# Where the expert stage turns its rows: TensorE blocks through PSUM, or VectorE blocks of 32 by 32 in SBUF

## The chip, the core and the metric

One core of one Trainium2 chip runs the whole kernel as one program. TensorE (PE in the profile; its weight loads are PEld) multiplies, VectorE (DVE) and ScalarE (ACT) work on elements, GpSimd (POOL) issues the indexed transfers and SyncE (SP) the plain ones. The metric is the device time of one execution in microseconds (us), lower is better; the figure for a kernel is the median over runs.

## What is computed

A graph layer, a linear-attention mixer and then a mixture of experts over 1250 rows of 768 float32 numbers. Only the last matters here:

```python
probs = jax.nn.softmax(x @ router_w, axis=-1)
gates, idx = jax.lax.top_k(probs, TOPK_ROUTED)      # 8 experts, 2 for each row
gates = gates / jnp.sum(gates, axis=-1, keepdims=True)
g = jax.nn.silu(jnp.einsum('bsd,edh->bseh', x, w_gate))
u = jnp.einsum('bsd,edh->bseh', x, w_up)
expert_out = jnp.einsum('bseh,ehd->bsed', g * u, w_down)
routed = jnp.einsum('bse,bsed->bsd', dense_g, expert_out)
return alpha * shared + (1.0 - alpha) * routed
```

## The kernel before

The expert stage is the last third of the kernel, from about 1028 us of the span on. The rows picked for the experts have been written to DRAM in order of expert (`expert_in`), in 23 tiles (NTM) of 128 slots; the two halves of a tile (HP = 64 slots) may belong to two experts, whose weights lie in two sets of SBUF buffers.

What TensorE does with tile j (`tile` in `ffn_pe`): the gate product into banks 0 and 1, the up product into banks 2 and 3, then the down product into banks 4 and 5. Each product has two column blocks of 384 and six row blocks of 128 (KD = 6), and each of these is a pair of matmuls, one for each half of the slots (`product`). In gate and up the column block is the outer loop, in down the row block is. So a tile has 36 pairs, six times six: two sixths for gate (blocks 0 and 1), two for up, and two for down (rows 0 to 2, then 3 to 5). Down needs the gated rows as columns and gate needs the fetched rows as columns, and TensorE makes both by transposes: `h_transposes(j, 0)` turns the first half of the gated rows `hh` into bank 0, `x_transposes(j + 1)` the next tile's fetched rows `xgb` into banks 6 and 7, `h_transposes(j, 1)` the second half into bank 1. They stand between up and down, twelve of 128 by 128 in all. Three sorts of copies take them to SBUF: L885 (ScalarE, two for each tile, to `xgT`), L896 (ScalarE, to the first half of `hT`) and L1165 (VectorE, to the second half).

ScalarE further fetches the rows of tile j + 2 (`load_x`, L880) and applies Silu to the gate blocks (L894). VectorE multiplies the two up blocks by that (`take_h`, L1160) and adds the down result into rows of the output that GpSimd fetches (`add_rows`, L1173, two instructions for each half h). On GpSimd the two halves of a tile go strictly one after the other, since both may name the same output row: gather half 0 (L698), wait for the addition, scatter (L702), and only when that has landed gather half 1, wait for its addition, scatter. An addition waits for its gather, and half 0 also for the down product.

All engines run in order. VectorE's program is written out tile by tile: two `take_h`, the copy L1165, `add_rows(j, 0)`, `add_rows(j, 1)`. Weights of another expert are fetched by SyncE (L661) as soon as the last tile that uses the old ones is through gate, up or down. The names of semaphores that show below: `h_ready` (multiplication done), `hT_psum`, `hT_copied_act`, `hT_copied_dve` (turned and copied), `slot_xT_sb` (turned rows of a tile in SBUF), `out_rows_in` (gather landed), `y_psum` (down done), `y_added` (additions done).

Of the kernel before, what the change touches and what calls it, by code (L numbers as in the profile page):

```python
# [31 lines left out]
P = 128  # L32
# [24 lines left out]
def gps_layer(nc, x, src, dst, norm_g, norm_b, W1, a_src1, a_dst1, b1, W2, a_src2, a_dst2, b2, Wu, bu,  # L57
# [25 lines left out]
    with ExitStack() as ctx:  # L83
        def sem(name):
            return ctx.enter_context(nc.semaphore(name))
# [472 lines left out]
        s_g = sem("gate_psum")  # L558
        s_up = sem("up_psum")
        s_slot_xT = sem("slot_xT_psum")  # L560
        s_ht = sem("hT_psum")
        s_y = sem("y_psum")
        s_silu = sem("silu_ready")
        s_xTs = sem("slot_xT_sb")
        s_h = sem("h_ready")
        s_hTa = sem("hT_copied_act")
        s_hTs = sem("hT_copied_dve")
        s_yd = sem("y_added")
        s_last = sem("last_step")
        s_fout = sem("out_rows_written")  # L570
# [141 lines left out]
        def ffn_pe(pe, xf_turn):  # L712
# [85 lines left out]
                            ins.then_inc((s_g, s_up, s_y)[2 * i + k], 1)  # L798
                    ins.then_inc(s_slot_xT, 1)

            def h_transposes(j, b, i):

                pe.wait_ge(s_h, 2 * j + 1 + i)
                for k in range(3):
                    ins = tp.transpose(ps[i][:, k * P:(k + 1) * P], hh[:, b, (3 * i + k) * P:(3 * i + k + 1) * P], ident)
                ins.then_inc(s_ht, 1)

            def product(bank, frm, b, k, i, n):

                for h in range(2):  # L810
# [4 lines left out]
            def tile(j, b):  # L815

                loads = pe.value_load(loads_i[0:1, bass.ds(j, 1)], min_val=32, max_val=16 * (NB1 + 2))
                pe.wait_ge(s_xTs, 2 * j + 2)
                for m in range(2):
                    pe.wait_ge(s_ew[m], loads)  # L820
                    for i in range(2):
                        for k in range(KD):
                            ins = product(2 * m + i, xgT, b, k, m, i)
                        ins.then_inc((s_g, s_up)[m], 1)
                h_transposes(j, b, 0)
                if not (isinstance(j, int) and j == NTM - 1):
                    x_transposes(j + 1, 1 - b)
                else:
                    pe.wait_ge(s_last, 1)
                    tp.transpose(ps[6][:, 0:P], rows_f.to_broadcast([P, P]), ident).then_inc(s_slot_xT, 1)  # L830
                h_transposes(j, b, 1)
                pe.wait_ge(s_ew[2], loads)
                if not (isinstance(j, int) and j == 0):
                    pe.wait_ge(s_yd, 4 * j)
                for k in range(KD):
                    if k == 0:
                        pe.wait_ge(s_hTa, j + 1)
                    if k == 3:
                        pe.wait_ge(s_hTs, j + 1)
                    for o in range(2):  # L840
                        ins = product(4 + o, hT, b, k, 2, o)
                ins.then_inc(s_y, 1)
# [8 lines left out]
        def ffn_act(act):  # L851
            def take_xf(t):
                act.wait_ge(s_xt, 2 * (NT + t) + 1)
                sc.activation(xfT[:, 0:3, t * T:(t + 1) * T], ps[4][:, 0:3 * T].rearrange("p (k n) -> p k n", k=3),
                              ACT.Copy).then_inc(s_xta, 1)

            act.wait_ge(s_stats, 5)
            sc.activation(std[0:T, 0:5], mv[0:T, 0:5, 1], ACT.Sqrt, bias=epst[0:T]).then_inc(s_std, 1)
            for t in range(3):
                take_xf(t)  # L860
            act.wait_ge(s_stats, 6)
            sc.activation(std[0:T, 5:NT], mv[0:T, 5:NT, 1], ACT.Sqrt, bias=epst[0:T]).then_inc(s_std, 1)
            for t in range(NT):
                if t + 3 < NT:
                    take_xf(t + 3)
                act.wait_ge(s_sgp, t + 1)
                sc.activation(sg_s[0:T, t], ps[t % 2][0:T, 0:HS], ACT.Silu).then_inc(s_ssil, 1)
            act.wait_ge(s_exin, 1)
            sc.activation(ex[0:T], ex[0:T], ACT.Exp)
            sc.activation(ex2[0:T], ex2[0:T], ACT.Exp).then_inc(s_exout, 1)  # L870
            act.wait_ge(s_sgb, 16)
            sc.activation(alpha[0:T], lg[0:T, :, NE], ACT.Sigmoid, bias=sgb[0:T]).then_inc(s_exout, 1)
            for t in range(NT):
                act.wait_ge(s_shT, t + 1)
# [12 lines left out]

            def tile(j, b):
                last = isinstance(j, int) and j == NTM - 1
                if not (isinstance(j, int) and j + 2 >= NTM):  # L890
                    load_x(j + 2, b)
                for i in range(2):
                    act.wait_ge(s_g, 2 * j + 2 + i)
                    sc.activation(gs[:, b, i * 384:(i + 1) * 384], ps[i][:, 0:384], ACT.Silu).then_inc(s_silu, 1)  # L894
                act.wait_ge(s_ht, 2 * j + 1)
                sc.activation(hT[:, b, 0:3].rearrange("p k n -> p (k n)"), ps[0][:, 0:384], ACT.Copy).then_inc(s_hTa, 1)  # L896
                if not last:
                    take_x(j + 1, 1 - b)
                else:
                    act.wait_ge(s_h, 2 * j)  # L900
                    act.wait_ge(s_y, j + 2)
                    sc.activation(gs[:, 1, 0:384], ps[4][:, 0:384], ACT.Copy).then_inc(s_last, 1)

            act.wait_ge(s_rows, 16 * 2 * NT)
            load_x(0, 0)
            load_x(1, 1)
            take_x(0, 0)
            over_tiles(act, tile)

        def ffn_dve(dve, step, add_out, mean_var):  # L910
# [241 lines left out]
            for t in range(NT - 3, NT):  # L1152
                shared_out(t)

            def take_h(j):
                b = j % 2
                for i in range(2):
                    dve.wait_ge(s_silu, 2 * j + 1 + i)
                    dve.wait_ge(s_up, 2 * j + 2 + i)
                    dv.tensor_tensor(hh[:, b, i * 384:(i + 1) * 384], ps[2 + i][:, 0:384], gs[:, b, i * 384:(i + 1) * 384],  # L1160
                                     ALU.mult).then_inc(s_h, 1)

            def take_hT(j):
                dve.wait_ge(s_ht, 2 * j + 2)
                dv.tensor_copy(hT[:, j % 2, 3:6].rearrange("p k n -> p (k n)"), ps[1][:, 0:384]).then_inc(s_hTs, 1)  # L1165

            def add_rows(j, h):
                if h == 0:
                    dve.wait_ge(s_y, j + 2)
                dve.wait_ge(s_accin, 16 * (2 * j + h + 1))  # L1170
                for o in range(2):
                    cols = accb[0:HP, h, o * 384:(o + 1) * 384]
                    stt(out=cols, in0=ps[4 + o][HP * h:HP * h + HP, 0:384], scalar=slot_info[0:HP, j, h, 0:1], in1=cols,  # L1173
                        op0=ALU.mult, op1=ALU.add).then_inc(s_yd, 1)

            def last_rows():

                dve.wait_ge(s_slot_xT, 2 * NTM + 1)
                dv.tensor_scalar(same, ps[6][:, 0:P], rows_f[:, 0:1], info_last[:, 0:1], ALU.is_equal, ALU.mult).then_inc(s_last, 1)
                dve.wait_ge(s_h, 2 * NTM - 2)  # L1180
                dve.wait_ge(s_y, NTM + 1)
                dv.tensor_copy(gs[:, 1, 384:768], ps[5][:, 0:384]).then_inc(s_last, 1)
                dve.wait_ge(s_accin, 16 * (2 * NTM - 1))
                for o in range(2):
                    dve.wait_ge(s_last, 5 + o)
                    cols = accb[:, 0, o * 384:(o + 1) * 384]
                    dv.tensor_tensor(cols, cols, ps[7 - o][:, 0:384], ALU.add).then_inc(s_yd, 1)

            for j in range(NTM - 1):
                take_h(j)  # L1190
                take_hT(j)
                if j == 0:
                    dve.wait_ge(s_infoin, 32)
                    dv.tensor_copy(rows_f, info_last[:, 1:2].bitcast(I32)).then_inc(s_last, 1)
                    dve.wait_ge(s_last, 1)
                add_rows(j, 0)
                add_rows(j, 1)
            take_h(NTM - 1)
            take_hT(NTM - 1)
            last_rows()  # L1200


# [1301 lines left out]
```

## Time and profile before

| | us |
|---|---|
| median of 3 runs | 1628.32 |
| lowest, highest | 1626.89, 1630.79 |
| span of the profiled execution, first to last instruction | 1625.5 |

The span is 2.8 us below the median; what a sum makes of the span is added to the median. In the profile a line of a timeline gives the start and the duration of merged instructions of one line of code, and in brackets how long the engine had been idle and what ended that. TensorE's durations overlap each other, since matmuls are pipelined: the distance between starts is what counts there.

### The profile page before, as it was taken

What the parts mean: (1) busy time and instruction counts of PE and PEld (TensorE: products, weight loads), DVE (VectorE), ACT (ScalarE), POOL (GpSimd) and SP (SyncE); (2) the same over time, 40 slices, a digit from 0 to 9 for tenths busy, and PEclk for the clock granted to TensorE, in tenths of its full rate; (3) what the DMA queues carried; (4) which work ended last, traced back from release to release, by engine and by line L of the source; (5) the groups of instructions that cost most, each with busy time, mean ns of one, the idle gap of its engine ahead of it and who ended that gap; (6) DMA issues with size and microseconds to landing.
All of it is one profiled execution on the core that took longest, in us unless ns stands there. A gap on an engine that the chain in (4) does not pass through costs nothing.

```text
span 1625.5 us, 21891 instructions
## 1 busy us (share of the span) xinstructions
PE 1541.0 (95%) x8438; PEld 1021.0 (63%) x8439; DVE 820.7 (50%) x1552; ACT 335.3 (21%) x493; POOL 252.9 (16%) x236
## 2 busy tenths in 40 slices
PE   5999999999989999999879999899999999999996
PEld 3566666557779999999876555444444444444442
DVE  8655457988867889984997243111111111111111
ACT  3321111002222345560481210100000000001000
POOL 1187810000000000000000037011111111111111
PEclk9999999999999999999999999999999999999998
DMA  9900010000004536213111337925629211613450
GB/s 269 344 2 2 2 62 1 1 1 2 1 19 121 140 80 190 59 24 85 46 33 59 146 69 161 328 66 188 222 55 320 92 48 53 213 40 112 153 203 21
DMA packets 85339, 163.81 MB, mean 101 GB/s; under 512 B 18874, under 2 KB 48816, under 8 KB 85001
## 3 DMA queue, kind: packets, MB, share of 16 engines
q1 hardware_dynamic: 66903, 119.07, 22.6%
q0 software_dynamic: 12096, 23.27, 6.3%
q10 hardware_dynamic: 6258, 20.40, 4.5%
q8 instruction: 48, 0.79, 0.2%
q14 instruction: 34, 0.28, 0.1%
HBM read 127.75 MB, written 37.56 MB: 102 GB/s over the span
## 4 chain that ended last, share of the span: by engine, by line
PE 66%; DVE 12%; POOL 8%; issue 6%; DMA 5%; SPq 1%; DVEq 1%; ACT 1%; POOLq 0%
PE bank L811 31%; PE bank L1636 7%; POOL slot_table L1332 7%; PE bank L1674 6%; PE bank L1538 5%; PE bank L1595 3%; PE bank L721 2%; DVE arena L2396 2%; PE bank L1474 2%; DVE arena L2365 2%; PE bank L1722 1%; DMA arena<-in_L_ffn_w_down_dram 1%; DMA expert_in<-arena 1%; POOL expert_in L679 1%; DVE arena L2341 1%
## 5 line engine op out<-in xcount | busy, mean ns | idle before, releaser
L811 PE MATMUL bank<-arena 128*64 128x384 f32 x3312 | 541.1, 488 | 3.7 <-DMA arena<-in_L_ffn_w_down_dram 3.1
L811 PEld LDWEIGHTS bank<-arena 128*64 128x64 f32 x3312 | 237.1, 137 | 296.0 <-issue 291.8
L1173 DVE SCALAR_TENSOR_TENSOR arena<-bank,arena 64x384 f32<-64x384 f32 x88 | 50.3, 610 | 355.2 <-DMA arena<-out_dram,arena 200.7
L1674 PE MATMUL bank<-arena 125*125 125x198 f32 (+1 forms) x1200 | 188.9, 317 | 13.5 <-DVE arena L2365 13.3
L1674 PEld LDWEIGHTS bank<-arena 125*125 125x125 f32 x1200 | 182.1, 191 | 18.2 <-DVE arena L2365 17.9
L1636 PE MATMUL bank<-arena 128*125 128x192 f32 x960 | 161.9, 326 | 0.0
L1636 PEld LDWEIGHTS bank<-arena 128*125 128x125 f32 x960 | 156.1, 188 | 0.2
L1332 POOL DMA_INDIRECT slot_table<-arena x80 | 110.7, 1384 | 93.8 <-issue 93.8
L2202 DVE TENSOR_TENSOR arena<-arena,bank 125x417 f32 x186 | 109.4, 588 | 27.1 <-PE bank L1474 18.9
L672 POOL MEMSET arena<- 1x2500 f32 x1 | 2.2, 2179 | 597.0 <-DVE arena L2348 597.0
L2396 DVE SCALAR_TENSOR_TENSOR arena<-arena 125x1250 f32<-125x1250 f32 x60 | 90.8, 1514 | 4.2 <-ACT arena L1911 4.2
L1538 PE MATMUL bank<-arena 128*125 128x396 f32 x240 | 92.9, 496 | 0.0
L894 ACT ACTIVATE arena<-bank 128x384 f32<-128x384 f32 x46 | 22.6, 492 | 338.8 <-PE bank L811 338.8
L1924 ACT ACTIVATE arena<-arena 125x1250 f32<-125x1250 f32 x60 | 74.7, 1245 | 83.0 <-DVE arena L2396 81.5
L1595 PE MATMUL bank<-arena 128*128 128x250 f32 x360 | 89.7, 374 | 1.7 <-DVE arena L2255 1.7
L2365 DVE SCALAR_TENSOR_TENSOR arena<-arena 125x1250 f32<-125x1250 f32 x60 | 87.1, 1453 | 0.9 <-PE bank L1674 0.9
L2341 DVE CUSTOM_DVE_ANT_0 arena<-arena 125x1250 bf16<-125x1250 bf16 x60 | 86.6, 1454 | 0.0
L702 POOL DMA_INDIRECT out_dram<-arena x44 | 40.4, 918 | 295.9 <-DVE arena L1173 283.1
L1911 ACT ACTIVATE arena<-arena 125x1250 f32<-125x1250 f32 x60 | 79.5, 1335 | 27.0 <-DMA arena<-score_rows 19.4
L1422 PE MATMUL bank<-arena 128*125 128x384 f32 x240 | 82.5, 497 | 0.0
L1450 PE MATMUL bank<-arena 128*125 128x384 f32 x240 | 80.4, 487 | 0.0
L1160 DVE TENSOR_TENSOR arena<-bank,arena 128x384 f32<-128x384 f32 x46 | 25.6, 558 | 99.2 <-PE bank L811 98.9
(302 smaller groups left out, 1564.6 us busy)
## 6 DMA issues: line engine op xcount, KB each, us to landing
arena<-in_L_ffn_w_gate_dram SPq DMA_DIRECT2D x9, 2304.0 KB, 8.9
arena<-in_L_ffn_w_up_dram SPq DMA_DIRECT2D x9, 2304.0 KB, 10.3
arena<-in_L_ffn_w_down_dram SPq DMA_DIRECT2D x9, 2304.0 KB, 8.8
arena<-score_rows ACTq DMA_DIRECT2D x18, 585.9 KB
expert_in<-arena SPq DMA_DIRECT2D x23, 384.0 KB, 10.2
arena<-expert_in ACTq DMA_DIRECT2D x23, 384.0 KB, 3.7
arena<-in_L_mix_w_qkv_dram SPq DMA_DIRECT2D x2, 2304.0 KB, 17.2
xn_columns<-arena SPq DMA_DIRECT2D x1, 3750.0 KB, 15.6
```

Source lines behind the costliest of these rows:

```text
L811: ins = tp.matmul(ps[bank][HP * h:HP * h + HP, 0:384], frm[:, b, k, HP * h:HP * h + HP], ew[h][i][:, k, n * 384:(n + 1) * 384], start=(k = ...
L1332: pl.indirect_dma_start(table_dram[:, :], bass.IndirectOffsetOnAxis(ap=slot_i[0:T, c:c + 1], axis=0), vhw[0:T, NTB * TC + c:NTB * TC + c + ...
L1422: ins = tp.matmul(ps[i % 2][0:T, 0:384], xnT[:, k, t * T:(t + 1) * T], wkv[:, 0, k, hf * 384:(hf + 1) * 384], start=(k == 0), stop=(k == K ...
L1450: ins = tp.matmul(ps[2 + hf][0:T, 0:384], xnT[:, k, t * T:(t + 1) * T], wkv[:, 1, k, hf * 384:(hf + 1) * 384], start=(k == 0), stop=(k == ...
L1538: ins = tp.matmul(ps[q % 4][0:T, 0:2 * VW], xnT[:, k, t * T:(t + 1) * T], w12x[:, k, 2 * hf:2 * hf + 2, :], start=(k == 0), stop=(k == KD ...
L1595: ins = tp.matmul(ps[q % 2][:, 0:QN], wq[:, k, mb * P:(mb + 1) * P], xnT[:, k, g * QN:(g + 1) * QN], start=(k == 0), stop=(k == KD - 1))
L1636: ins = tp.matmul(ps[side_bank(u)][0:T, 0:FW], frm[:, k, t * T:(t + 1) * T], wchunk[:, c % 2, k, :], start=(k == 0), stop=(k == KD - 1))
L1674: ins = tp.matmul(ps[bank][0:T, c * width:(c + 1) * width], ptile[0:T, j % NPT, dt * T:(dt + 1) * T], values(n - first, st), start=(st == ...
L2202: dv.tensor_tensor(o, o, ps[6 + j % 2][0:T, 0:G], ALU.add).then_inc(s_acc, 1)
L2341: step(dv.tensor_tensor_reduce(junk[0:T, dt % 2], mask[0:T, dt], srowb[0:T, n % 2], 1.0, -3.0e38, ALU.add, ALU.max, smax[0:T, dt:dt + 1]))
L2365: stt(out=ptile[0:T, j % NPT], in0=tbuf[0:T, j % NTB3], scalar=1.0, in1=counts[0:T, st, 0:N], op0=ALU.min, op1=ALU.mult).then_inc(s_pt, 1)
L2396: stt(out=tbuf[0:T, j % NTB3], in0=abbuf[0:T, n % 2, 1], scalar=ssrc[:, st:st + 1], in1=tbuf[0:T, j % NTB3], op0=ALU.add, op1=ALU.max).the ...
```

## The change

Of tile 0 the fetched rows are still turned by TensorE and copied by ScalarE. All others, and all gated rows, are turned by VectorE, 32 by 32 blocks at a time, from SBUF to SBUF: an instruction takes one strip of 32 partitions (rows r*32 on) and, of each 128 columns, the block number f, and writes to partitions f*32 on. For a strip there are four such instructions, for 128 rows sixteen: 32x96 elements each for half of the gated rows (3 blocks), 32x192 for the fetched rows (6 blocks). TensorE's transposes and the copies L885 (but for tile 0), L896 and L1165 are gone.

VectorE's tile j now is: multiply, 16 turns, multiply, 16 turns, the 16 turns of the fetched rows of tile j + 2 (`turn_x`), `add_rows(j, 0)`, `add_rows(j, 1)`. The down product's first half waits for `hT_sb` at the first 16 turns, its second half at the second 16.

```diff
             def tile(j, b):
...
-                h_transposes(j, b, 0)
-                if not (isinstance(j, int) and j == NTM - 1):
-                    x_transposes(j + 1, 1 - b)
...
-                h_transposes(j, b, 1)
                 pe.wait_ge(s_ew[2], loads)
...
                 for k in range(KD):
-                    if k == 0:
-                        pe.wait_ge(s_hTa, j + 1)
-                    if k == 3:
-                        pe.wait_ge(s_hTs, j + 1)
+                    if k % 3 == 0:
+                        pe.wait_ge(s_hTs, 2 * j + 1 + k // 3)
...
+            Q = 32
+
+            def turn_blocks(to, rows, r):
+
+                for f in range(P // Q):
+                    frm = rows[r * Q:(r + 1) * Q].rearrange("p (k f c) -> p f k c", f=P // Q, c=Q)[:, f]
+                    ins = dv.transpose(to[f * Q:(f + 1) * Q, :, r * Q:(r + 1) * Q], frm)
+                return ins
...
                     dv.tensor_tensor(hh[:, b, i * 384:(i + 1) * 384], ps[2 + i][:, 0:384], gs[:, b, i * 384:(i + 1) * 384],
                                      ALU.mult).then_inc(s_h, 1)
...
+                    dve.wait_ge(s_h, 2 * j + 1 + i)
+                    for r in range(P // Q):
+                        ins = turn_blocks(hT[:, b, 3 * i:3 * i + 3], hh[:, b, i * 384:(i + 1) * 384], r)
+                    ins.then_inc(s_hTs, 1)
+
+            def turn_x(j):
+                b = j % 2
+                dve.wait_ge(s_xg[b], 16 * (j // 2 + 1))
+                for r in range(P // Q):
+                    ins = turn_blocks(xgT[:, b], xgb[:, b], r)
+                ins.then_inc(s_xTd, 1)
...
+            turn_x(1)
             for j in range(NTM - 1):
                 take_h(j)
-                take_hT(j)
                 if j == 0:
...
+                if j + 2 < NTM:
+                    turn_x(j + 2)
                 add_rows(j, 0)
                 add_rows(j, 1)
```

VectorE, one tile of the middle of the stage (here L1160 multiplies, L1165 copies the turned half, L1173 adds; x2 is two instructions in a row). Before:

```order
L1160 TENSOR_TENSOR arena<-bank,arena 128x384 [waits up_psum,silu_ready] x2
L1165 COPY arena<-bank 128x384 [waits hT_psum]
L1173 SCALAR_TENSOR_TENSOR arena<-bank,arena 64x384 [waits out_rows_in,y_psum]
L1173 SCALAR_TENSOR_TENSOR arena<-bank,arena 64x384
L1173 SCALAR_TENSOR_TENSOR arena<-bank,arena 64x384 [waits out_rows_in]
L1173 SCALAR_TENSOR_TENSOR arena<-bank,arena 64x384
```

In the changed kernel (L1158 multiplies, L1150 turns, L1178 adds):

```order
L1158 TENSOR_TENSOR arena<-bank,arena 128x384 [waits up_psum,silu_ready]
L1150 STREAM_TRANSPOSE arena<-arena 32x3x32 [waits h_ready]
L1150 STREAM_TRANSPOSE arena<-arena 32x3x32 x15
L1158 TENSOR_TENSOR arena<-bank,arena 128x384 [waits up_psum,silu_ready]
L1150 STREAM_TRANSPOSE arena<-arena 32x3x32 [waits h_ready]
L1150 STREAM_TRANSPOSE arena<-arena 32x3x32 x15
L1150 STREAM_TRANSPOSE arena<-arena 32x6x32 [waits slot_rows_in0]
L1150 STREAM_TRANSPOSE arena<-arena 32x6x32 x15
L1178 SCALAR_TENSOR_TENSOR arena<-bank,arena 64x384 [waits out_rows_in,y_psum]
L1178 SCALAR_TENSOR_TENSOR arena<-bank,arena 64x384
L1178 SCALAR_TENSOR_TENSOR arena<-bank,arena 64x384 [waits out_rows_in]
L1178 SCALAR_TENSOR_TENSOR arena<-bank,arena 64x384
```

One copy has gone, and 48 turns have come in, 16 of them between the two multiplications and 32 between the second one and the additions.

TensorE from the up product on to the next gate product, at the same place. Before:

```order
L811 MATMUL bank<-arena 64x384 [waits expert_w1_in]
L811 MATMUL bank<-arena 64x384 x23
L805 MATMUL bank<-arena 128x128 [waits h_ready]
L805 MATMUL bank<-arena 128x128 x2
L796 MATMUL bank<-arena 128x128 [waits slot_rows_in0]
L796 MATMUL bank<-arena 128x128 x5
L805 MATMUL bank<-arena 128x128 [waits h_ready]
L805 MATMUL bank<-arena 128x128 x2
L811 MATMUL bank<-arena 64x384 [waits hT_copied_act,y_added,expert_w2_in]
L811 MATMUL bank<-arena 64x384 x11
L811 MATMUL bank<-arena 64x384 [waits hT_copied_dve]
L811 MATMUL bank<-arena 64x384 x11
```

In the changed kernel (`product` is L803):

```order
L803 MATMUL bank<-arena 64x384 [waits expert_w1_in]
L803 MATMUL bank<-arena 64x384 x23
L803 MATMUL bank<-arena 64x384 [waits hT_sb,y_added,expert_w2_in]
L803 MATMUL bank<-arena 64x384 x11
L803 MATMUL bank<-arena 64x384 [waits hT_sb]
L803 MATMUL bank<-arena 64x384 x11
```

Down now stands right behind up, and each of its halves waits for VectorE.

## Rows read from the trace of the kernel before

**Rows 1.** The page, part 1: busy time, share of the span, instructions.
```profile
PE 1541.0 (95%) x8438; PEld 1021.0 (63%) x8439; DVE 820.7 (50%) x1552; ACT 335.3 (21%) x493; POOL 252.9 (16%) x236
```

**Rows 2.** Timeline of PE: start, us, engine, line, tiles, count, [idle before]; one tile.
```profile
1150.41 23.44 PE L811 MATMUL bank<-arena 128*64 128x384 f32 x144
1173.78 0.55 PE L805 MATMUL bank<-arena 128*128 128x128 f32 x3
1174.16 0.82 PE L796 MATMUL bank<-arena 128*128 128x128 f32 x6
1174.82 0.49 PE L805 MATMUL bank<-arena 128*128 128x128 f32 x3
1175.24 23.44 PE L811 MATMUL bank<-arena 128*64 128x384 f32 x144
```

**Rows 3.** Timeline of DVE, one tile: additions of both halves, then the two multiplications.
```profile
1183.25 1.14 DVE L1173 SCALAR_TENSOR_TENSOR arena<-bank,arena 64x384 f32<-64x384 f32 x2 [7.34 <-PE bank L811]
1192.50 1.15 DVE L1173 SCALAR_TENSOR_TENSOR arena<-bank,arena 64x384 f32<-64x384 f32 x2 [8.12 <-DMA arena<-out_dram,arena]
1194.93 0.56 DVE L1160 TENSOR_TENSOR arena<-bank,arena 128x384 f32<-128x384 f32 x1 [1.27 <-PE bank L811]
1198.80 0.56 DVE L1160 TENSOR_TENSOR arena<-bank,arena 128x384 f32<-128x384 f32 x1 [3.31 <-PE bank L811]
```

**Rows 4.** Timeline of DVE, instructions queued with no wait between them: earlier stages.
```profile
223.53 0.35 DVE L2227 COPY arena<-bank 64x192 f32<-64x192 f32 x1
223.80 0.14 DVE L2228 COPY arena<-bank 64x3 f32<-64x3 f32 x1
223.96 0.36 DVE L2227 COPY arena<-bank 64x192 f32<-64x192 f32 x1
224.24 0.16 DVE L2228 COPY arena<-bank 64x3 f32<-64x3 f32 x1
...
951.12 0.15 DVE L1023 TENSOR_SCALAR arena<-arena 125x7 f32<-125x7 f32 x1
951.19 0.15 DVE L1024 TENSOR_SCALAR arena<-arena 125x7 f32<-125x7 f32 x1
```

**Rows 5.** Groups by line and shape: DVE from SBUF to SBUF; busy us, mean ns.
```profile
L2259 DVE COPY arena<-arena 125x80 f32<-125x80 f32 x1 | 0.2, 241 | 0.0
L1034 DVE TENSOR_TENSOR arena<-arena 125x196 f32<-125x196 f32 x1 | 0.4, 362 | 0.0
```

**Rows 6.** Timeline of DVE: the seven additions of half 1 that waited longest.
```profile
1121.29 1.15 DVE L1173 SCALAR_TENSOR_TENSOR arena<-bank,arena 64x384 f32<-64x384 f32 x2 [11.40 <-DMA arena<-out_dram,arena]
...
1170.28 1.15 DVE L1173 SCALAR_TENSOR_TENSOR arena<-bank,arena 64x384 f32<-64x384 f32 x2 [10.73 <-DMA arena<-out_dram,arena]
...
1248.88 1.15 DVE L1173 SCALAR_TENSOR_TENSOR arena<-bank,arena 64x384 f32<-64x384 f32 x2 [14.84 <-DMA arena<-out_dram,arena]
...
1272.56 1.15 DVE L1173 SCALAR_TENSOR_TENSOR arena<-bank,arena 64x384 f32<-64x384 f32 x2 [9.74 <-DMA arena<-out_dram,arena]
...
1422.56 1.16 DVE L1173 SCALAR_TENSOR_TENSOR arena<-bank,arena 64x384 f32<-64x384 f32 x2 [10.74 <-DMA arena<-out_dram,arena]
...
1521.41 1.15 DVE L1173 SCALAR_TENSOR_TENSOR arena<-bank,arena 64x384 f32<-64x384 f32 x2 [10.26 <-DMA arena<-out_dram,arena]
...
1571.43 1.15 DVE L1173 SCALAR_TENSOR_TENSOR arena<-bank,arena 64x384 f32<-64x384 f32 x2 [10.62 <-DMA arena<-out_dram,arena]
```

**Rows 7.** Timeline of PE around the longest of these waits.
```profile
1224.91 23.44 PE L811 MATMUL bank<-arena 128*64 128x384 f32 x144
1250.68 0.90 PE L805 MATMUL bank<-arena 128*128 128x128 f32 x3 [2.33 <-DVE arena L1160]
...
1253.43 23.68 PE L811 MATMUL bank<-arena 128*64 128x384 f32 x144
```

**Rows 8.** Stretches: us, busy PE, PEld, DVE, ACT, POOL, then PEclk, DMA share, GB/s.
```profile
1248.00:1250.60 2.60, 0.35 (x4) 0.00 (x0) 1.68 (x4) 0.00 (x0) 0.00 (x0) 0.99 0.92 238
1250.60:1253.40 2.80, 2.72 (x12) 2.42 (x12) 0.49 (x2) 1.48 (x3) 0.92 (x1) 0.50 1.02 410
1253.40:1256.50 3.10, 3.10 (x19) 1.42 (x20) 0.56 (x1) 0.00 (x0) 0.00 (x0) 0.91 1.04 408
```

More of the change, by code:

```diff
@@ L560, in gps_layer @@
         s_slot_xT = sem("slot_xT_psum")
-        s_ht = sem("hT_psum")
         s_y = sem("y_psum")
@@ L565, in gps_layer @@
         s_h = sem("h_ready")
-        s_hTa = sem("hT_copied_act")
-        s_hTs = sem("hT_copied_dve")
+        s_hTs = sem("hT_sb")
+        s_xTd = sem("slot_xT_turned")
         s_yd = sem("y_added")
@@ L799, in x_transposes @@
                     ins.then_inc(s_slot_xT, 1)
[L801 to L806, printed above, removed]
             def product(bank, frm, b, k, i, n):
@@ L817, in tile @@
                 loads = pe.value_load(loads_i[0:1, bass.ds(j, 1)], min_val=32, max_val=16 * (NB1 + 2))
-                pe.wait_ge(s_xTs, 2 * j + 2)
+                if isinstance(j, int) and j == 0:
+                    pe.wait_ge(s_xTs, 2)
+                else:
+                    pe.wait_ge(s_xTd, j)
                 for m in range(2):
@@ L824, in tile @@
                         ins.then_inc((s_g, s_up)[m], 1)
-                h_transposes(j, b, 0)
-                if not (isinstance(j, int) and j == NTM - 1):
-                    x_transposes(j + 1, 1 - b)
-                else:
+                if isinstance(j, int) and j == NTM - 1:
                     pe.wait_ge(s_last, 1)
                     tp.transpose(ps[6][:, 0:P], rows_f.to_broadcast([P, P]), ident).then_inc(s_slot_xT, 1)
-                h_transposes(j, b, 1)
                 pe.wait_ge(s_ew[2], loads)
@@ L890, in tile @@
                 if not (isinstance(j, int) and j + 2 >= NTM):
+                    if not (isinstance(j, int) and j == 0):
+                        act.wait_ge(s_xTd, j)
                     load_x(j + 2, b)
@@ L893, in tile @@
                     act.wait_ge(s_g, 2 * j + 2 + i)
+                    if i == 0 and not (isinstance(j, int) and j < 2):
+                        act.wait_ge(s_h, 2 * j - 2)
                     sc.activation(gs[:, b, i * 384:(i + 1) * 384], ps[i][:, 0:384], ACT.Silu).then_inc(s_silu, 1)
[L895 to L899, printed above, removed]
+                if last:
                     act.wait_ge(s_h, 2 * j)
@@ L1161, in take_h @@
                                      ALU.mult).then_inc(s_h, 1)
-            def take_hT(j):
-                dve.wait_ge(s_ht, 2 * j + 2)
-                dv.tensor_copy(hT[:, j % 2, 3:6].rearrange("p k n -> p (k n)"), ps[1][:, 0:384]).then_inc(s_hTs, 1)
+                    dve.wait_ge(s_h, 2 * j + 1 + i)
[8 more added lines that the diff above has]
+                ins.then_inc(s_xTd, 1)
             def add_rows(j, h):
@@ L1176, in last_rows @@
             def last_rows():
-                dve.wait_ge(s_slot_xT, 2 * NTM + 1)
+                dve.wait_ge(s_slot_xT, 3)
                 dv.tensor_scalar(same, ps[6][:, 0:P], rows_f[:, 0:1], info_last[:, 0:1], ALU.is_equal, ALU.mult).then_inc(s_last, 1)
@@ L1198, in ffn_dve @@
             take_h(NTM - 1)
-            take_hT(NTM - 1)
             last_rows()
```

## The prediction

> **What bounds the kernel now.** I read the page first: TensorE is busy 95% of the span, VectorE 50% [rows 1]. The share says only that TensorE is the one to relieve; what relief is worth is read in the stage itself. There the timeline of TensorE is regular: a stretch of products starts at 1150.41 and the next at 1175.24, so a tile takes 24.83 us, with the twelve transposes in the 1.46 us between 1173.78 and 1175.24 [rows 2]. TensorE never idles in such a tile. The timeline of VectorE gives the products' pace: the two multiplications start 3.87 us apart, which is one sixth of a tile's products [rows 3], so the products take 6 x 3.87 = 23.2 us and the transposes, with what they keep the queue from doing, 24.83 - 23.2 = 1.6 us. That is all that the change can take from TensorE.
>
> VectorE's own timeline is the one to study, since it gets the work. Its additions of half 0 start when down ends (1183.25), those of half 1 9.25 us later (1.13 of work and 8.12 of waiting for the scatter and the next gather), and end at 1193.65; the first multiplication starts at 1194.93, 11.68 after the down product's end, because up's first block is ready then [rows 3]. So VectorE has only 1.3 us of air between the last addition and the first multiplication, and in 7 of 22 tiles none: there the wait of half 1 is 9.74 to 14.84 us [rows 6].
>
> **What is removed.** 23 tiles' transposes on TensorE, all but the fetched rows of tile 0; taken alone 1.6 x 22 = 35 us. The copies on ScalarE are hidden now and give nothing; the 0.56 us copy on VectorE went to nobody's wait but the down product's second half.
>
> **What is added: the price of a turn.** 32 instructions of 32x96 and 16 of 32x192 for each tile, in the second half of a chain that TensorE waits for. The trace has no turn; the bounds come from the nearest rows.
> Duration: SBUF to SBUF, 125x80 took 241 ns and 125x196 took 362 ns [rows 5], that is 1.04 ns for each further column and 158 ns fixed; 96 columns are 258 ns, 192 are 358 ns.
> Distance between starts: that depends on what VectorE may overlap. Two instructions of 7 columns on the same partitions start 0.07 us apart although each lasts 0.15, and a 192-column copy lets the next one start after 0.27 of its 0.35 us. But where the copies go over from partitions 0 to 63 to partitions 64 to 127, the next one starts only when the last has ended: 223.80 + 0.14, next at 223.96 [rows 4]. So overlapped a turn costs 0.27 - (192 - 96) x 0.00104 = 0.17 us for 96 columns and 0.27 for 192; not overlapped 0.258 + 0.02 = 0.28 and 0.38. In `turn_blocks` f is the inner loop, so every instruction writes to another strip of 32 partitions than the one before it. I take the row with the change of partitions, since it is the nearer one. On top of that a block can hardly leave before its last of 32 columns has come in, 32 x 1.04 = 33 ns more, in full or not at all; I take a third of that: **0.29 us for 96 columns, 0.39 for 192**, and keep 0.28 and 0.31 for the range.
>
> The Trainium skill says the same of the overlap, and it speaks against this change: in "VectorE: DVE Perf Modes", section "Two Vector instructions with no wait between them", an instruction whose output starts in another quadrant (32 partitions) than the last output into that memory is held until all earlier ones are finished. Its section "The three transpose paths" gives 311 ns for 128x128 bf16 on VectorE. An estimate from that figure would be 311 less 32 x 1.04 = 278 ns, with the gap 0.30 us for 96 columns, and the sum below would be 10 us higher.
>
> **A tile of the changed kernel.** Count from H, the end of the last turn of the gated rows, which lets TensorE do the second half of down.
> Turning the next fetched rows: 16 x 0.39 = 6.24, to H + 6.26. Down ends as VectorE sees it at H + 4.2 (0.06 for the signal, 3.87 for the sixth, 0.26 for the end of the pipeline), so `turn_x` delays the additions of half 0 by 2.1 us.
> Additions of half 0 at 6.26, of half 1 9.25 later at 15.51, end 16.66.
> The first multiplication could start 11.68 after down's end, at 15.87; VectorE is free at 16.69, 0.82 later.
> Each half now is 0.56 + 0.04 (its own wait) + 16 x 0.29 = 5.24 us; two are 10.48.
> Next H: 16.69 + 10.48 = **27.17 us a tile, against 24.83: 2.34 more**. VectorE's chain, not TensorE, sets the pace, as 5.24 is more than the 3.87 between two blocks. TensorE sees it as two gaps: about 2.6 us before down and 1.4 us before its second half.
>
> **What the long waits add.** In the 7 tiles of [rows 6] the wait is 11.19 us on average instead of 8.12. Before, the air and TensorE's slack took most of that; only the longest reached TensorE, where a period of 28.52 (1224.91 to 1253.43) was 3.69 too long [rows 7]. Now the multiplications stand behind the additions with no air, so all of it counts: 7 x 3.07 = 21.5, less the 3.7 already in the time. VectorE is in order, so a transfer that the down product does not need holds up the turning that it does need.
>
> **Sum.** 22 tiles x 2.34 = 51.5; + 21.5 - 3.7 = 69.3. The first tile (where the additions also stand behind a turn) gives some 2 us more, two shorter waits and the last tile, which has no fetched rows to turn, some 2 less. The span goes from 1625.5 to about 1695, the median from 1628.3 to **1697 us**.
>
> **The clock.** After TensorE idled 2.33 us the granted clock was 0.50 for 2.8 us, the 1.2 GHz level, and 0.91 right after [rows 7, 8]; the whole tile lost 3.69, so the clock about 1.4. The new gap of 2.6 us is as long. I cost this at nothing: the slow stretch would be the first half of down, behind which TensorE waits another 1.4 us for the second 16 turns anyway. If that cover fails it is 22 x 1.4 = 31 us more.
>
> **Rivals.**
> (a) The turns overlap, or only a change of the strip that is read counts (one in four: 0.17 + 0.028 = 0.20 at most). For it: the queued pairs at 0.07 and 0.27 [rows 4], and that this row changes the partitions read and written together, so it does not say which one counts. At 0.17 a half takes 0.56 + 0.04 + 2.72 = 3.3 us, less than 3.87, so the turns are hidden and 22 x 1.6 = 35 us are saved, also the 3.7 of the old stall; but in the 7 long tiles the first multiplication comes some 2 us late and the first half of down 1.7, 12 us: 1628 - 27 = 1601, up to 1612 at 0.20. That is the faster side. It decides at a turn of about 0.22 us: every 0.01 us of a turn costs 32 x 0.01 before down and 16 x 0.01 before the additions, 0.48 a tile, 10 us in all, and 7 steps down from 0.29 the 69 us are used up. Chance 0.13.
> (b) `turn_x` costs nothing where it stands and the long waits shrink, since the additions start 2 us later and meet less of the weight fetch beside them; only the turns themselves count: 2 x 5.24 - 2 x 3.87 + some 0.4 for the signals = 3.1 a tile, less 1.6, times 22 = 33 us, 1661. Against it: 6.24 us is longer than down. Chance 0.11.
> (c) The clock's cover fails: 1697 + 31 = 1728. Chance 0.09.
> (d) A block goes through at half the rate, so 96 columns cost 0.38 and 192 cost 0.58: H + 9.3, additions to 19.65, two halves of 6.68: 33.1 a tile, 8.3 more, 22 x 8.3 + 18 = 200, 1828. No row speaks for it. Chance 0.05.
>
> **How the numbers follow.** The forecast has 0.60: turns of 0.28 to 0.31 give 1687 to 1718. The range leaves out (a) and (d): from 1655, a little below (b), to 1735, a little above (c). Measured against no change, about 0.2% can be told (3 us). Faster 0.12, same 0.02 (a turn of just 0.22), slower 0.86.
>
> **What would show it.** The turns' durations and the distance between their starts, 0.29 against 0.17, decide most. Then TensorE's waits: twice a tile for VectorE, 2.6 and 1.4 us, periods of 27.2, and of 30 in the seven tiles with long waits; additions of half 0 with VectorE busy right before them, not waiting for down; the granted clock at 0.5 behind the first gap. I am wrong if the turns start less than 0.25 us apart, if the additions of half 0 still wait for the down product, or if the stage's tiles are under 24.8 us.

## The result and the profile after

The changed kernel takes 1706.6 us (median of 4 runs, 1702.8 to 1707.9) where the kernel before takes 1627.6 on the same chips: 1.048 times as long, 95% interval 1.046 to 1.050. The profiled execution spans 1705.5 us, 80.0 more than before.

The page, busy time. TensorE's busy time is the same as in [rows 1] although 270 matmuls are gone, since in 15 of the 22 tiles the first half of down ran at the lower clock (TensorE's rows of such tiles are 24.8 to 26.4 us long, where 4.09 + 19.57 = 23.66 is full speed); its share is 90%. VectorE has 316 us more:

```profile
PE 1540.8 (90%) x8168; PEld 1001.4 (59%) x8169; DVE 1137.1 (67%) x2617; ACT 307.0 (18%) x426; POOL 252.7 (15%) x236
```

The chain that ended last, by line, where the turns of VectorE now lead and the landings of gathers and scatters follow TensorE's lines:

```profile
DVE arena L1150 15%; PE bank L803 7%; POOL slot_table L1338 6%; PE bank L1680 6%; PE bank L1642 6%; DMA arena<-out_dram,arena 5%; PE bank L1544 4%; DMA out_dram<-arena 4%; PE bank L1601 3%; PE bank L720 2%; SPq L379 2%; DVE arena L2402 2%; DVE arena L1178 2%; PE bank L1480 2%; DVE arena L2371 2%
```

Groups by shape in the expert stage: the two sorts of turns (busy us, mean ns of one).

```profile
L1150 DVE STREAM_TRANSPOSE arena<-arena 32x96 f32<-32x96 f32 x736 | 199.0, 270 | 10.8
L1150 DVE STREAM_TRANSPOSE arena<-arena 32x192 f32<-32x192 f32 x352 | 130.1, 370 | 8.3 <-DMA arena<-expert_in 3.3
```

One tile in VectorE's timeline, to be laid beside [rows 3] (the row of 10.67 us holds the second 16 turns of gated rows and the 16 of fetched rows):

```profile
1189.71 0.56 DVE L1158 TENSOR_TENSOR arena<-bank,arena 128x384 f32<-128x384 f32 x1
1190.31 4.52 DVE L1150 STREAM_TRANSPOSE arena<-arena 32x96 f32<-32x96 f32 x16
1194.86 0.56 DVE L1158 TENSOR_TENSOR arena<-bank,arena 128x384 f32<-128x384 f32 x1
1195.45 10.67 DVE L1150 STREAM_TRANSPOSE arena<-arena 32x96 f32<-32x96 f32 x32
1206.15 1.14 DVE L1178 SCALAR_TENSOR_TENSOR arena<-bank,arena 64x384 f32<-64x384 f32 x2
1215.61 1.15 DVE L1178 SCALAR_TENSOR_TENSOR arena<-bank,arena 64x384 f32<-64x384 f32 x2 [8.32 <-DMA arena<-out_dram,arena]
1216.89 0.56 DVE L1158 TENSOR_TENSOR arena<-bank,arena 128x384 f32<-128x384 f32 x1
```

Read it from the first multiplication (1189.71) to the next tile's (1216.89): 27.18 us, and VectorE idles for long only in the 8.32 us of waiting for the gather of half 1. The additions of half 0 start with no idle time, so they no longer wait for the down product. Sixteen turns take 4.52 us: 15 distances and one duration of 0.27, so a distance of 0.283; the multiplications stand 5.15 us apart, where TensorE's blocks are 3.87 apart. TensorE, to be laid beside [rows 2]:

```profile
1222.07 4.09 PE L803 MATMUL bank<-arena 128*64 128x384 f32 x24 [1.42 <-DVE arena L1150]
1227.22 19.57 PE L803 MATMUL bank<-arena 128*64 128x384 f32 x120 [1.06 <-DVE arena L1150]
1252.98 25.73 PE L803 MATMUL bank<-arena 128*64 128x384 f32 x144 [6.20 <-DVE arena L1150]
1287.22 25.68 PE L803 MATMUL bank<-arena 128*64 128x384 f32 x144 [8.51 <-DVE arena L1150]
```

Two waits for the turns in a tile, before down and before its second half (in the last two rows the first half of down ran at the lower clock and swallowed the second wait). From the start of down in tile 0 to that in tile 22 it is now 1048.75 to 1680.29, 631.5 us, against 1049.64 to 1601.15, 551.5 us, before: all of the 80 us lie there.

### The profile page after: what moved, and what is told of

The parts are those of the page before. It is cut to its first block, busy times and chain, and to the rows that moved or that the text cites. A ratio compares the mean times of both kernels' runs of the same rounds, so it can differ in the third digit from the quotient of the medians.

```text
span 1705.5 us, 22326 instructions
## 1 busy us (share of the span) xinstructions
PE 1540.8 (90%) x8168; PEld 1001.4 (59%) x8169; DVE 1137.1 (67%) x2617; ACT 307.0 (18%) x426; POOL 252.7 (15%) x236
## 3 DMA queue, kind: packets, MB, share of 16 engines
q1 hardware_dynamic: 66903, 119.07, 21.5%
## 4 chain that ended last, share of the span: by engine, by line
PE 37%; DVE 30%; DMA 11%; issue 9%; POOL 8%; SPq 3%; DVEq 1%; ACT 1%; POOLq 0%
DVE arena L1150 15%; PE bank L803 7%; POOL slot_table L1338 6%; PE bank L1680 6%; PE bank L1642 6%; DMA arena<-out_dram,arena 5%; PE bank L1544 4%; DMA out_dram<-arena 4%; PE bank L1601 3%; PE bank L720 2%; SPq L379 2%; DVE arena L2402 2%; DVE arena L1178 2%; PE bank L1480 2%; DVE arena L2371 2%
## 5 line engine op out<-in xcount | busy, mean ns | idle before, releaser
L803 PE MATMUL bank<-arena 128*64 128x384 f32 x3312 | 570.6, 507 | 88.4 <-DVE arena L1150 86.3
L803 PEld LDWEIGHTS bank<-arena 128*64 128x64 f32 x3312 | 244.2, 143 | 414.0 <-issue 313.3
L1150 DVE STREAM_TRANSPOSE arena<-arena 32x96 f32<-32x96 f32 (+1 forms) x1088 | 329.1, 303 | 19.1 <-DMA arena<-expert_in 3.3
L1178 DVE SCALAR_TENSOR_TENSOR arena<-bank,arena 64x384 f32<-64x384 f32 x88 | 50.3, 610 | 218.9 <-DMA arena<-out_dram,arena 213.6
L2208 DVE TENSOR_TENSOR arena<-arena,bank 125x417 f32 x186 | 109.4, 588 | 27.2 <-PE bank L1480 18.9
```

The costliest lines, as they stand in the source:

```text
L803: ins = tp.matmul(ps[bank][HP * h:HP * h + HP, 0:384], frm[:, b, k, HP * h:HP * h + HP], ew[h][i][:, k, n * 384:(n + 1) * 384], start=(k = ...
L1150: ins = dv.transpose(to[f * Q:(f + 1) * Q, :, r * Q:(r + 1) * Q], frm)
L2208: dv.tensor_tensor(o, o, ps[6 + j % 2][0:T, 0:G], ALU.add).then_inc(s_acc, 1)
```

## The experiments

My theory after this: VectorE's chain sets the pace. A turn is held (it starts only when the one before has ended) whenever the strip of 32 partitions changes; the gated rows' turns make two blocks 10.3 us long in place of 7.7; the fetched rows' turns delay the additions of half 0 by 2 us and with them the gather of half 1. What the forecast had not foreseen is that the waits for the gather of half 1 grew: 213.6 us over the 22 tiles, 196.4 before. I first put that down to the fetch of the expert rows on ScalarE, which the change had let slip from behind TensorE's transposes to the end of the gate product.

**load_late: the fetch of rows back at its old place.**

```diff
                     if not (isinstance(j, int) and j == 0):
                         act.wait_ge(s_xTd, j)
+                        act.wait_ge(s_hTs, 2 * j)
                     load_x(j + 2, b)
```

> The changed kernel, with the fetch of the rows of tile j + 2 on ScalarE held back until the gated rows of tile j - 1 are turned; that is where it stood before the change, whereas the change had let it move up to the end of the gate product, beside the gather of half 1. Theory: that fetch is what made the additions of half 1 wait 9.71 us on average in place of 8.93 (213.6 and 196.4 us over 22 tiles). With it gone from there the waits fall back to 8.1 in a tile without a fetch of weights, the sum by about 17 us, and the time from 1707 to about 1690. Rival: the gathers are slower because VectorE's turns keep GpSimd from making its descriptors, or because the additions as such stand later beside the weights; then the waits stay at 9.7 and the time at 1707.

Measured: 1707.4 us, 1.047 of before (1.043 to 1.051): nothing gained, that theory fell as a sum. Its trace shows why. In tiles without a fetch of weights the wait did fall to 8.0, as in [rows 3], but the total stayed at 212.1, since others grew. In the seven tiles in which gate weights are fetched (one of them is also among the seven of [rows 6]), the waits for half 1 sum to 62.6 us before, 75.3 in the changed kernel and 79.1 in load_late; in the other fifteen to 133.8, 138.4 and 133.0. So the fetch of rows did cost about 5 us, which load_late gave back; the larger part of the growth lies with the gate weights. Timelines of SyncE, GpSimd and VectorE of load_late in one tile where gate weights are fetched:

```profile
1440.33 0.39 SPq L660 DMA_DIRECT2D arena<-in_L_ffn_w_gate_dram  x1
```
```profile
1440.14 0.95 POOL L697 DMA_INDIRECT arena<-out_dram,arena  x1 [2.85 <-DMA out_dram<-arena]
```
```profile
1447.76 1.15 DVE L1179 SCALAR_TENSOR_TENSOR arena<-bank,arena 64x384 f32<-64x384 f32 x2 [12.21 <-DMA arena<-out_dram,arena]
```

The gather was issued from 1440.14 to 1441.09, the fetch of the gate weights from 1440.33; the gather landed at 1447.76, when the additions start, 6.7 us after its issue had ended. In the changed kernel the same gather had 0.6 us of lead (1445.19 against 1445.79) and landed at 1449.57, 3.4 us after the end of its issue:

```profile
1445.79 0.39 SPq L660 DMA_DIRECT2D arena<-in_L_ffn_w_gate_dram  x1
```
```profile
1445.19 0.95 POOL L697 DMA_INDIRECT arena<-out_dram,arena  x1 [2.85 <-DMA out_dram<-arena]
```

The two traces have fourteen gathers of half 1 near a fetch of gate weights, and they fall in line. Counted from the start of the gather's issue to the start of the additions, six gathers with 0.2 to 0.3 us of lead took 6.5 to 7.6 us, two with 0.4 to 0.5 took 4.6 and 5.2, two with 0.6 took 4.3 and 4.4, and two with 1.3 and 1.9 took 3.4, as undisturbed ones do. The two that were issued after the fetch took 7.0 and 7.8.

So the second theory: it is the additions' delay. The gather of half 1 goes out 5.7 us after the additions of half 0 begin. With those 2.1 us late that is 7.8 us after down's end, and the gate product, which starts with down's end, lasts 7.75. Its end lets both the gate weights and the rows of the next tile be fetched, and the gather runs beside one or both.

**add_first: the same 48 turns, the fetched rows' behind the additions of half 0.**

```diff
-                if j + 2 < NTM:
-                    turn_x(j + 2)
                 add_rows(j, 0)
+                if j + 2 < NTM:
+                    turn_x(j + 2)
                 add_rows(j, 1)
```

> The changed kernel with the 16 turns of the fetched rows moved behind the additions of half 0, into VectorE's wait for the gather of half 1. Theory (the fetch of rows alone was not the cause; the additions' delay of 2.1 us is, since it puts the gather of half 1 beside the fetch of the gate weights and of the rows, which start when the gate product ends): the additions of half 0 wait for the down product again, the gather goes out 5.7 us after down's end, ahead of those fetches, the 6.2 us of turns hide in the 8.1 us of wait, and a tile is 4.2 + 11.68 + 10.3 = 26.2 us: about 1670, as with the gated rows alone on VectorE (1673). Rival: VectorE's total work counts, wherever the turns stand; then it stays near 1700.

Measured: 1675.8 us, 1.029 (1.027 to 1.031). Moving one call takes back 31 us of the 79. The rival, that VectorE's total counts wherever it stands, is out. VectorE's timeline:

```profile
1307.55 1.13 DVE L1178 SCALAR_TENSOR_TENSOR arena<-bank,arena 64x384 f32<-64x384 f32 x2 [4.36 <-PE bank L803]
1308.61 6.10 DVE L1150 STREAM_TRANSPOSE arena<-arena 32x192 f32<-32x192 f32 x16
1316.68 1.15 DVE L1178 SCALAR_TENSOR_TENSOR arena<-bank,arena 64x384 f32<-64x384 f32 x2 [1.98 <-DMA arena<-out_dram,arena]
1319.22 0.56 DVE L1158 TENSOR_TENSOR arena<-bank,arena 128x384 f32<-128x384 f32 x1 [1.39 <-PE bank L803]
...
1333.68 1.14 DVE L1178 SCALAR_TENSOR_TENSOR arena<-bank,arena 64x384 f32<-64x384 f32 x2 [4.20 <-PE bank L803]
```

The additions wait for the down product again (4.36), the turns fill the wait for the gather, of which 1.98 us are left, and half 1 follows half 0 by 9.13 us, before 9.25. The tile is 26.13 us (1307.55 to 1333.68), 1.3 more than before. Two causes are in the 31 us. The distances between the additions of the two halves sum to 225.6 us over the 22 tiles, where the changed kernel has 238.6 and the kernel before 221.3: that is 13. The rest, about 18, is that the turns of the fetched rows no longer stand in VectorE's chain. The gather of this tile was issued from 1313.27 to 1314.22, beside the turns, and landed 3.4 us after 1313.27 as before, so turns on VectorE do not as such slow a gather, which was the other rival of load_late.

**add_first_load_late: both edits.**

> The same, and the fetch of rows held back as in load_late. Theory: the gathers then stand as before the change and the summed wait of half 1 with the turns in it is that of before, 196 us; 1665 to 1670, at most 5 us under add_first. Rival (the late fetch meets the weights of down instead, which is why load_late gained nothing): same as add_first or slower by up to 5.

Measured: 1671.6 us, 1.027 (1.024 to 1.030). The interval overlaps that of add_first (1.027 to 1.031); the 4 us between the medians are near the 5 that were expected at most, and are not shown to be more than noise. In the trace the distances between the two halves sum to 222.3 us, 3.3 less than in add_first.

**h_only: only the gated rows on VectorE.** The edit takes `turn_x` out and puts `x_transposes(j + 1)` and the copies L885 back between up and down.

> The gated rows are turned by VectorE as in the change, the fetched rows by TensorE and ScalarE as before. Theory: two halves cost 2 x 5.16 us against 2 x 3.87 between their blocks, and nothing stands before the additions of half 0; first multiplication 11.68 after down's end, so a tile is 4.2 + 11.68 + 10.32 = 26.2 us, 1.4 more than before: 22 x 1.4 = 30, and the seven long waits add some 9 after what they cost before. About 1667. Rival: the turns of the gated rows fit under the products and only those of the fetched rows hurt, then the time is that of before or a little less, 1610 to 1628.

Measured: 1673.4 us, 1.027 (1.026 to 1.029). The turns of the gated rows alone cost 45 us, and with those of the fetched rows in the wait (add_first) it is the same: there they are free, but they gain nothing either, since in h_only TensorE's transposes of the fetched rows stand in its wait for the gated ones. In one tile of h_only they start at 1323.68 and take 0.87 us, and TensorE still waits 0.62 us more for the turns before down starts at 1325.17; the tile is 26.15 us long, against 26.13 in add_first.

**x_only: only the fetched rows on VectorE, in the down product's time.**

```diff
                 take_h(j)
                 take_hT(j)
...
+                if j + 2 < NTM:
+                    turn_x(j + 2)
                 add_rows(j, 0)
                 add_rows(j, 1)
```

> The fetched rows are turned by VectorE, right after it has copied the second half of the gated rows and before its additions; the gated rows are turned by TensorE with copies as before. Theory: 16 turns take 6.2 us and start 0.7 us into the down product of 7.75 us, so they are hidden. TensorE loses 0.66 us of transposes but then waits for the multiplication and the copy of the gated rows that these covered, so it gains only about 0.3 us a tile: 22 x 0.3 = 6, about 1621. Rival: the turns delay the additions of half 0 here too and the chain of gathers behind them, then 2 us a tile in the seven long ones and a time over 1628.

Measured: 1624.6 us over 10 runs, 0.9976 of before (0.9960 to 0.9991), 0.24% faster, where about 0.4% was expected. VectorE's and TensorE's timelines:

```profile
1303.43 0.56 DVE L1183 COPY arena<-bank 128x384 f32<-128x384 f32 x1 [0.64 <-PE bank L806]
1303.90 6.11 DVE L1163 STREAM_TRANSPOSE arena<-arena 32x192 f32<-32x192 f32 x16
1311.33 1.13 DVE L1191 SCALAR_TENSOR_TENSOR arena<-bank,arena 64x384 f32<-64x384 f32 x2 [1.32 <-PE bank L812]
```
```profile
1302.04 0.55 PE L806 MATMUL bank<-arena 128*128 128x128 f32 x3
1302.85 0.55 PE L806 MATMUL bank<-arena 128*128 128x128 f32 x3 [0.26 <-DVE arena L1178]
1303.32 23.44 PE L812 MATMUL bank<-arena 128*64 128x384 f32 x144
```

The same sixteen turns in the same place of the program cost nothing here, with 1.32 us to spare, because nothing slow stands before them. TensorE now waits 0.26 us for the multiplication of the second block, which the transposes of the fetched rows had covered, so of their 0.66 us only 0.18 are left of a tile (24.65 between two groups in place of 24.83).

**write_strip_kept: four turns in a row write to one strip and read from four.**

```diff
-            def turn_blocks(to, rows, r):
+            def turn_blocks(to, rows, f):
 
-                for f in range(P // Q):
+                for r in range(P // Q):
```

> The changed kernel with the two loops of the turns exchanged: four turns in a row write to the same strip of 32 partitions and read from four different ones; in the change they read from one and write to four. Theory: a turn starts only when the one before has ended if either strip changes, so the distance stays 0.284 us and the time 1707. Rival: only a change of the strip that is written counts; then three of four turns start 0.17 us after the one before, a turn costs 0.20 on average, and the time is near 1615.

Measured: 1704.4 us, 1.046 (1.043 to 1.050), as the change. Sixteen turns take as long as there:

```profile
1217.03 4.52 DVE L1150 STREAM_TRANSPOSE arena<-arena 32x96 f32<-32x96 f32 x16
```

A change of the strip that is read holds a turn as much as one of the strip that is written.

**x_split: each turn of the fetched rows in two, on the same strips.**

```diff
+                    for f in range(P // Q):
+                        for g in range(2):
+                            frm = xgb[r * Q:(r + 1) * Q, b, g * 384:(g + 1) * 384].rearrange("p (k f c) -> p f k c", f=P // Q, c=Q)[:, f]
+                            ins = dv.transpose(xgT[f * Q:(f + 1) * Q, b, 3 * g:3 * g + 3, r * Q:(r + 1) * Q], frm)
```

> The changed kernel with each turn of the fetched rows (six blocks) made as two of three blocks, so that every second one reads and writes the same strips as the one before it. Theory: the distance is 0.284 us where a strip changes and 0.165 where none does, so 16 pairs take 16 x 0.45 = 7.2 us in place of 6.2 and the time is 1 us a tile longer, about 1730. Rival: turns never overlap, whatever strips they use; then all 32 stand 0.284 apart, 9.1 us, and 1770.

Measured in one run: 1732.2 us; the reading rests on the distances in its trace, not on that time. VectorE's timeline, 16 turns that all change strips and 32 of the same size of which every second does not:

```profile
1326.96 4.53 DVE L1150 STREAM_TRANSPOSE arena<-arena 32x96 f32<-32x96 f32 x16
1331.51 7.08 DVE L1172 STREAM_TRANSPOSE arena<-arena 32x96 f32<-32x96 f32 x32
```

All held, 32 turns would take 31 x 0.283 + 0.27 = 9.0 us; they take 7.1. A pair costs (7.08 - 0.27 + 0.283) / 16 = 0.443, so the turn that keeps its strips starts 0.443 - 0.283 = 0.16 us after the one before it, as rival (a) had it at 0.17. Turns do overlap; a full turn of 128 rows, built of one instruction for each pair of strips, cannot use it, since two instructions in a row always differ in the strip that they read or in the one that they write.

**x_only_early, x_only_k4, all_pe_k4: can the transposes that stay be hidden better?** In the first two only the fetched rows are on VectorE, between its two additions, and TensorE turns the first half of the gated rows inside up's second block (behind row block 2, in x_only_k4 behind 4) and the second half behind down's first:

```diff
                             ins = product(2 * m + i, xgT, b, k, m, i)
+                            if (m, i, k) == (1, 1, 2):
+                                h_transposes(j, b, 0)
...
                         ins = product(4 + o, hT, b, k, 2, o)
+                    if k == 0:
+                        h_transposes(j, b, 1)
```

> Only the fetched rows on VectorE, between its two additions. TensorE turns the gated rows, the first half in the middle of up's second block and the second half behind the first row block of down, so that their multiplication and copies are covered by products. Theory: TensorE loses nothing but six transposes, 0.8 us of the 1.6 a tile; 22 x 0.8 = 18, and the one old stall of 3.7 shrinks: about 1607, faster than both kernels. Rival: transposes between products of the same accumulation cost more than in a block, or the copies are late; then 1615 to 1625, as with x_only.

Measured: 1629.7 us, 1.001 (0.999 to 1.002): no gain, where 1607 was expected. A tile did shrink, to 24.47 us, but only by 0.36 and not by 0.8, since the two small groups cost 24.47 - 23.2 = 1.3 us; and TensorE now meets a late multiplication earlier. That takes back 10.1 - 2.3 = 7.8 us, as much as the 22 shorter tiles give. The waits of TensorE for VectorE's multiplication in the stage:

```profile
PE bank L806 <- DVE arena L1180: 10.1, 5, 4.9
```

> As x_only_early, but TensorE turns the first half of the gated rows two row blocks later, 1.3 us before the end of up, so that a multiplication that is late behind the additions holds up TensorE by 2.6 us less. In x_only_early a tile took 24.47 us (24.83 before, 24.65 in x_only), but TensorE waited 10.1 us for the multiplication in five tiles with long waits of the additions, 2.3 in the kernel before. Theory: the period stays 24.47, so 22 x 0.36 = 8 us are gained, and the waits fall to about 4 us; about 1620. Rival: the copy of the first half is then late for down, and a tile is as long as in x_only: 1625.

Measured: 1625.4 us over 12 runs, 0.9977 (0.9964 to 0.9990). The waits fell to 4.9 us, as expected, and the time only to that of x_only. The longest, 4.50 us, was followed by a slower stretch:

```profile
1252.38 0.55 PE L806 MATMUL bank<-arena 128*128 128x128 f32 x3 [4.50 <-DVE arena L1180]
1252.86 3.76 PE L812 MATMUL bank<-arena 128*64 128x384 f32 x12
...
1303.47 2.16 PE L812 MATMUL bank<-arena 128*64 128x384 f32 x12
```

Twelve matmuls took 3.76 us where they take 2.16 in the tile of the last row. That is 1.6 us. Add 2.6 more of waiting than before, and about 1.0 more than before for the slower stretch after the wait for weights in tile 0 (down's start to the next group of transposes is 25.78 us there and about 23.4 in a later tile; before, 24.81 and 23.37). Of the 7.9 us that the shorter tiles give, 2.7 are left; the spans differ by 2.1, the medians by 3.2. The forecast of 1620 had counted the shorter tiles whole, with none of the three against them.

In all_pe_k4 nothing is turned by VectorE: it is the kernel before, with the transposes of the gated rows at the places of x_only_k4 and those of the fetched rows still between up and down.

> No turn on VectorE: the kernel before with the transposes of the gated rows at the places of x_only_k4, those of the fetched rows behind up. It tells whether the gain of x_only_k4 comes from VectorE's turns or from the places. Theory: a group of three transposes between products costs 0.61 us (six in two groups 1.22 in x_only_early), six more about 0.8, so a tile is 23.25 + 2.0 = 25.3, slower than before by 0.4 x 22 = 9: about 1637. Rival: the places are what gains; then it is at or under 1625.

Measured: 1643.5 us, 1.009 (1.007 to 1.011). The places alone lose: a tile is 25.44 us (the two rows below). Small groups of transposes between products cost TensorE more than one large group. What x_only_k4 gained came from VectorE's turns of the fetched rows. TensorE's timeline, the group before up's last row block in two tiles:

```profile
1310.61 0.55 PE L805 MATMUL bank<-arena 128*128 128x128 f32 x3
...
1336.05 0.55 PE L805 MATMUL bank<-arena 128*128 128x128 f32 x3
```

## Why the prediction was right

It said 1697 with a range of 1655 to 1735; it is 1707. Step by step, in the stage's 22 tiles:

- **The price of a turn** was put at 0.29 and 0.39 us; it is 0.283 and 0.38 (16 in 6.10 us). The choice between the overlapped and the held row of [rows 4] decided the sign, and it was right: rival (a), 1601, needed 0.17. The third of a block's 33 ns that I added on top is there in size: a turn of 96 columns lasts 270 ns, 12 more than the 258 from [rows 5], and one of 192 lasts 370, 12 more than 358; whether the block is the cause is not shown. What was too high is the gap between a turn's end and the next one's start, 0.013 us and not the 0.02 of [rows 4]. The rule of the Trainium skill cited for it ("VectorE: DVE Perf Modes", "Two Vector instructions with no wait between them") holds here, for writing (the changed kernel) as for reading (write_strip_kept), and turns that keep both strips are not held (x_split). Taken together the price was some 0.2 us a tile too high, 5 us.
- **The pace.** Forecast 27.17 us for a tile with the ordinary wait; the tile shown above, with a wait of 8.32, took 27.2. VectorE's chain sets it, the additions of half 0 follow the turns with no idle time, as said. TensorE's two gaps were forecast at 2.6 and 1.4 us. Before down they are 1.4 to 2.9 behind an ordinary wait, shorter where the down before ran at the lower clock; before the second half it is 1.06, since the first half takes 4.09 us as TensorE sees it and not 3.87. Rival (b), in which `turn_x` costs nothing in its place, is wrong for the change and right for x_only: what decides is whether the gated rows' turns stand ahead of it.
- **The long waits.** This is the term that was mis-sized: the forecast had 22 x 8.12 + 21.5 = 200 us of waiting for the gathers of half 1, the trace has 213.6. The seven long waits of [rows 6] did not grow: 78.3 us before, 77.3 now. In those tiles the weights of down are fetched from down's end on, beside the scatter of half 0, and the gather of half 1 goes out 8.0 to 9.1 us after the additions of half 0 in place of 5.7 (7.7 to 8.8 in the changed kernel). The other fifteen did, forecast at 8.12 each, 121.8 in sum, and measured at 136.3 (118.0 before). That the additions start 2.1 us later was in the working, but I moved only VectorE's side of it. The gather of half 1 moves too, into the end of the gate product, beside the fetches of gate weights and rows. Rival (b) had this the wrong way round, as a relief. Shown by add_first, where the additions are on time, the gather leads the gate weights by about 2 us in six of the seven tiles, the distance of the two halves in an ordinary tile is 9.13 us again and their sum 13 us less; the fourteen gathers under load_late show it singly.
- **The clock.** Costed at nothing, with the wait before down's second half as cover. The loss came but was covered nearly whole: stretches around the gap before down of the tile at 1194.88,

```profile
1192.00:1195.00 3.00, 0.12 (x2) 0.12 (x4) 2.85 (x11) 0.00 (x0) 0.74 (x1) 0.63 0.30 66
1195.00:1198.00 3.00, 3.00 (x10) 1.12 (x12) 2.85 (x11) 0.00 (x0) 0.21 (x1) 0.50 0.24 66
1198.00:1201.00 3.00, 3.00 (x16) 1.27 (x14) 2.86 (x10) 0.00 (x0) 0.00 (x0) 0.73 0.00 0
1201.00:1204.00 3.00, 3.00 (x20) 1.26 (x18) 2.89 (x9) 0.00 (x0) 0.00 (x0) 1.00 0.00 0
```

  The granted clock is at 0.50, the 1.2 GHz level, at the start of down and back at 1.00 before the gate product. The wait before the second half was not the whole cover: this row of 144 matmuls took 25.76 us, 1.04 more than 4.09 + 1.06 + 19.57 = 24.72 with its wait at full speed, so the loss was about 2.1. The 1.04 went into time in which VectorE was still at its additions (0.82 us by the forecast) and the next multiplication came only some 0.1 us late. In the whole stage VectorE waited for TensorE before a first multiplication in only three middle tiles, 2.7 us in all, 1.07 of it in this one, whose down had started at 1343.83:

```profile
1366.46 0.56 DVE L1158 TENSOR_TENSOR arena<-bank,arena 128x384 f32<-128x384 f32 x1 [1.07 <-PE bank L803]
```

  Rival (c), 31 us, is out. After a gap of 1.42 us the first half of down took its full-speed 4.09 us (row at 1222.07). The gap's length alone does not tell: after 2.92 us (down at 1343.83) the clock was 0.50, after 2.93 us (down at 1399.28) it was 1.00 and the first half took 4.09. What made the difference is open.

Sum of the corrections: 69 - 5 + 14 + 3 = 81, measured 80. The forecast was close in part because a price a little too high stood against a wait that was too short.

## What to carry to other kernels

Before moving work to an engine that looks half idle, lay its timeline beside the one it serves, and ask whether the new work stands in a chain that someone waits for and what it stands behind: the same sixteen turns cost nothing behind a short copy (x_only) or in a wait for a transfer (add_first), and put off additions, gathers and multiplications where the engine had no air left. Price short instructions by the distance of their starts under the same change of partitions, not by their durations or by a queue that overlaps. And when a step starts later, move the transfers that it releases as well, and see what they then run beside.

## What the runs showed of the hardware

- A turn of a 32-partition strip of 96 float32 columns lasts 0.270 us, of 192 columns 0.370. At 96 columns one that changes the strip it reads or writes starts 0.283 us after the one before (0.382 at 192 columns); one that changes neither starts after 0.16.
- Gathers whose issue began 0.2 to 0.3 us ahead of a 2.3 MB fetch of weights landed 6.5 to 7.6 us after that beginning; with 0.6 us of lead over that fetch and a fetch of rows 4.3 and 4.4 us after it, and with 1.3 or more 3.4. The order within a microsecond is worth some 3 us of a wait.
- Transposes on TensorE cost by the group: twelve in one row 1.6 us of a tile, six in two separate groups 24.47 - 23.2 = 1.3, twelve in three groups 25.44 - 23.2 = 2.2.
- A gap of 2.92 us on TensorE was followed by a granted clock of 0.50, one of 2.93 us in the same trace by 1.00.
